# A graph layer on one NeuronCore: the next block's score chain moved forward in the edge stream, and the mixing work on k and v done tile by tile

## The reference, cut to what matters

```
# attention over edges, 4 heads of 64 features
z = s_self[:, edge_row] + s_neigh[:, edge_col]
e = where(z > 0, z, 0.2 * z) * adj_val
ex = exp(e - segment_max(e, edge_row)[edge_row])
alpha = ex / segment_sum(ex, edge_row)[edge_row]
out = relu(segment_sum(alpha * feat[edge_col], edge_row) + bias)
# mixing, 8 heads of 64
q, k, v = split(x @ w_qkv)
k, v = inst_norm(k), inst_norm(v)          # mean and variance over a head's 64 features
dots = einsum('bhnd,bhne->bhde', k, v)
mix = (einsum('bhnd,bhde->bhne', q, dots) / n) @ w_out + b_out
x = x + out + mix
```

## Time and profile before

| | |
|---|---|
| median of 3 runs | 2548.52 us |
| the profiled execution | 2553.18 us, its span 2551.4 us |
| weights of blocks 0 and 25 (exponents, L972) | at 615.71 and 1758.56 us |
| last add of the edge stream (L1387) | 1792.89 us |
| busy in the span | PE 1742.6, DVE 1735.7, ACT 1408.0, POOL 1367.9 us |
| mean granted TensorE clock | 0.801 |

### The profile page before, as it was taken

How to read it: one execution, slowest core, us unless ns; L and a number is a source line. 1 busy time by engine, 2 the same in 40 slices (tenths; PEclk the granted TensorE clock), 3 DMA queues, 4 the chain that set the end, 5 groups by cost and what they waited for, 6 DMA issues and landing times. The chain is left out here.

```text
span 2551.4 us, 39924 instructions
## 1 busy us (share of the span) xinstructions
PE 1742.6 (68%) x8110; PEld 1309.4 (51%) x8111; DVE 1735.7 (68%) x3888; ACT 1408.0 (55%) x4644; POOL 1367.9 (54%) x1293
## 2 busy tenths in 40 slices
PE   3788841146666656766676776767574699999965
PEld 1444421023444444544454454544464699999954
DVE  6988999974776766777766556566883344444468
ACT  2555543315767757768776865868441244444434
POOL 2444410017777666666777666660177466666521
PEclk9899975566766877777878787878555799999988
DMA  6333420025554544454655444440629233333354
GB/s 200 132 141 146 168 85 0 0 82 157 159 158 152 167 152 144 142 180 123 186 158 174 131 140 117 141 139 17 199 44 131 66 105 105 104 105 106 102 169 146
DMA packets 173333, 323.66 MB, mean 127 GB/s; under 512 B 34435, under 2 KB 108720, under 8 KB 173182
## 3 DMA queue, kind: packets, MB, share of 16 engines
q1 hardware_dynamic: 110750, 172.84, 21.0%
q0 software_dynamic: 54176, 140.57, 19.4%
q10 hardware_dynamic: 8256, 8.68, 1.7%
HBM read 248.04 MB, written 73.94 MB: 126 GB/s over the span
## 5 line engine op out<-in xcount | busy, mean ns | idle before, releaser
L953 POOL DMA_INDIRECT big<-feat_d,pair_idx x832 | 819.9, 985 | 360.2 <-issue 177.0
L980 ACT ACTIVATE big<-big 128x64 f32<-128x64 f32 x3328 | 800.3, 333 | 0.8
L1081 PE MATMUL wide<-big 128*128 128x260 f32 x1664 | 637.6, 510 | 105.4 <-DVE big L1387 87.0
L1387 DVE TENSOR_TENSOR big<-big,wide 128x260 f32 x832 | 352.1, 423 | 341.8 <-PE wide L1081 262.2
L1081 PEld LDWEIGHTS wide<-big 128*128 128x128 f32 x1664 | 351.8, 244 | 176.5 <-ACT big L980 110.2
L313 ACT ACTIVATE big<-big 128x896 f32<-128x896 f32 (+2 forms) x153 | 136.9, 895 | 170.1 <-DVE big L538 155.1
L2068 PEld LDWEIGHTS p_h<-xT,w_sb 128*128 128x128 f32 x1808 | 221.7, 194 | 5.7
L2068 PE MATMUL p_h<-xT,w_sb 128*128 128x128 f32 x1808 | 222.1, 277 | 0.0
L2079 PE MATMUL p_o<-w_sb,hT 128*128 128x256 f32 x904 | 213.9, 379 | 1.1 <-DVE w_sb L2017 1.1
L1958 POOL DMA_INDIRECT moe_d<-x_out,x_to x113 | 134.6, 1191 | 135.6 <-DVE x_idx L1997 95.7
L278 POOL TENSOR_SCALAR xn<-X,mean,rstd 128x256 f32<-128x256 f32 x49 | 97.7, 1994 | 188.3 <-PE p_t L616 154.3
(11 more groups left out here) (327 smaller groups left out, 2853.2 us busy)
## 6 DMA issues: line engine op xcount, KB each, us to landing
big<-code_d SPq DMA_DIRECT2D x52, 512.0 KB, 4.0
kv_d<-big SPq DMA_DIRECT2D x49, 512.0 KB, 2.7
X<-kv_d SPq DMA_DIRECT2D x12, 2048.0 KB, 11.5
big<-in_L_ffn_w_dram SPq DMA_DIRECT2D x32, 512.0 KB, 10.5
b_sb<-in_L_ffn_b_dram SPq DMA_DIRECT2D x113, 128.0 KB, 3.0
big<-feat_d,pair_idx POOLq DMA_INDIRECT x832
big<-moe_d SPq DMA_DIRECT2D x7, 1792.0 KB, 10.0
feat_d<-feat_sb SPq DMA_DIRECT2D x49, 130.0 KB, 2.7
```

The lines of the kernel that those rows point to most:

```text
L953: nc.gpsimd.indirect_dma_start(out=rows[:, n // SB % RB, n % SB, :], out_offset=None, in_=m["feat_d"], in_offset=bass.IndirectOffsetOnAxis ...
L980: ins = nc.scalar.activation(rows[:, b, s, cols], rows[:, b, s, cols], ACT.Copy, scale=rows[:, b, s, HF + h:HF + h + 1])
L1081: nc.tensor.matmul(sums[s % RING][:, 0:HF + H], onehot[:, s // GP % 2, s % GP, :], rows[:, b, s, :], start=True, stop=True).then_inc(summe ...
L1387: nc.vector.tensor_tensor(of, of, sums[s % RING][:, 0:HF + H], ALU.add).then_inc(added, 1)
```

## The change

The chain for block k+1 begins in block k at add 6 in place of add 22. With it move the steps of all three engines: PE's four transposing steps go behind sums 8, 13, 17 and 21 (before: 23, 25, 26 and 27), `head` on ACT goes from slot 12 to slot 4 and the squares from slot 6 to slot 12. `sum_self` is done a block earlier, at slot 25 of the block before. The sums of squares, the scaling of v and the wait of each dot product now go one tile at a time, each of the first two as up to four instructions at four places. `first_hot` is a new one-row one-hot, so that `turn_arg` no longer reads the large one-hot buffer. `carry_f` and `carry_b` now live in `pens`.

```
 # ACT step
-                scale(k, b, range(0, 6))
+                scale(k, b, range(0, 4))
+                if there(k + 1):
+                    head(k + 1)
+                scale(k, b, range(4, 12))
                 if products:
                     squares_of(k, b, turn)
-                scale(k, b, range(6, 12))
-                if there(k + 1):
-                    head(k + 1)
                 scale(k, b, range(12, SB))
 # PE
-                nc.tensor.matmul(p_arg[:, HS:HS + H], onehot[0:1, 0, 0, :], drop[:], start=True, stop=True)
+                nc.tensor.matmul(p_arg[:, HS:HS + H], first_hot[:], drop[:], start=True, stop=True)
-                if i == 0:
-                    pe.wait_ge(v_scaled, k + 1)
+                pe.wait_ge(v_scaled, k * DB + (i + 1))
-                    i = (s - 8) // 2
-                    if s % 2 == 0 and i in batch(k - 1):
-                        dots(k - 1, 1 - b, i)
+                    if s - 9 in batch(k - 1):
+                        dots(k - 1, 1 - b, s - 9)
-                    if s in (8, 11, 14) and (s - 8) // 3 < len(groups(k)):
+                    if s in (9, 12, 15) and (s - 9) // 3 < len(groups(k)):
 # PE step, in the loop over s, behind sum s, its look-ups and mixing
+                    if s == 8:
+                        turn_z(k + 1)
+                    elif s == 13:
+                        turn_ends(k + 1)
+                    elif s == 17:
+                        turn_carry(k + 1)
+                    elif s == 21:
+                        turn_arg(k + 1)
 # DVE
+                wait_turn(dve, arg_turned, k)
+                nc.vector.tensor_tensor(first_hot[:], lane_p[0:1, :], pair_rel[0:1, ds(k * SB, 1)].to_broadcast([1, P]), ALU.is_equal)
-                nc.vector.tensor_reduce(var[:, 0:n * 2 * MH], squares[:, 0:n, :].rearrange("p t (h o) -> p t h o", o=64),
-                                        AX, ALU.add).then_inc(var_made, 1)
+                nc.vector.tensor_reduce(var[:, heads], squares[:, i, :].rearrange("p (h o) -> p h o", o=64), AX, ALU.add).then_inc(var_made, 1)
+            def scale_v(k, b, i):
+                v = kv[:, b, i, INNER:].rearrange("p (h o) -> p h o", o=64)
+                nc.vector.tensor_tensor(v, v, rkv[:, i, :].unsqueeze(2).to_broadcast([P, MH, 64]), ALU.mult).then_inc(v_scaled, 1)
 # DVE mixing: roots ahead of add 1, scale_v(i) ahead of add 2 + i, sum_squares(i) ahead of add 16 + 2 i
 # DVE step
-                if more:
-                    sum_self(k + 1)
                 fade_row(k, tile)
-                adds(range(0, 8))
+                adds(range(0, 3))
+                if more:
+                    heads(k + 1)
+                adds(range(3, 6))
+                if more:
+                    scores(k + 1, 1 - b, turn + b)
+                adds(range(6, 8))
                 select(k, 2)
-                adds(range(8, 11))
+                adds(range(8, 10))
+                if more:
+                    local_max(k + 1)
+                adds(range(10, 11))
                 if later:
                     turn_hot(2 * k + 5)
-                adds(range(11, 16))
+                adds(range(11, 14))
+                if more:
+                    carries(k + 1)
+                adds(range(14, 16))
                 select(k, 3)
+                adds(range(16, 19))
+                if more:
+                    arguments(k + 1)
+                adds(range(19, 25))
+                if more:
+                    select(k + 1, 0)
+                if later:
+                    sum_self(k + 2)
...
```

More of the change, by code:

```diff
@@ L719, in edge_stream @@
     run_b = sb("run_b", [1, H * (SB + 1) + 1])
-    carry_f, carry_b = sb("carry_f", [1, H, SB]), sb("carry_b", [1, H, SB])
-    drop = sb("drop", [1, H])
+    carry_f, carry_b = [pens[:].rearrange("u d h s -> u d (h s)")[:, d, 0:HS].rearrange("u (h s) -> u h s", h=H) for d in range(2)]
+    drop, first_hot = sb("drop", [1, H]), sb("first_hot", [1, P])
     wide = [ps(f"wide{i}", [P, 1024]) for i in range(4)]
@@ L1062, in turn_carry, with add_up @@
                 wait_apart(pe, carry_made, k + 1, crossed)
[L1063 to L1064 removed]
+                nc.tensor.transpose(p_row[0:HS, 256:257], flat(carry_f), ident[0:1, 0:1])
+                nc.tensor.transpose(p_row[0:HS, 257:258], flat(carry_b), ident[0:1, 0:1]).then_inc(col_turned, 1)
             def turn_arg(k):
                 pe.wait_ge(drop_made, k + 1)
[L1068 removed]
                 wait_turn(pe, ex_made, 2 * k)
                 wait_apart(pe, arg_made, k + 1, crossed)
[L1071 removed]
+                nc.tensor.matmul(p_arg[:, HS:HS + H], first_hot[:], drop[:], start=True, stop=True)
                 nc.tensor.transpose(p_arg[:, 0:HS], arg[:], ident[:]).then_inc(arg_turned, 1)
[L1074 to L1084, removed]
+            def add_up(k, b, s):
+                n = k * SB + s
+                if s % GP == 0:
+                    pe.wait_ge(hot_made, k * (SB // GP) + (s // GP + 1))
+                pe.wait_ge(scaled, n + 1)
+                pe.wait_ge(added, n + 1)
+                nc.tensor.matmul(sums[s % RING][:, 0:HF + H], onehot[:, s // GP % 2, s % GP, :], rows[:, b, s, :],
+                                 start=True, stop=True).then_inc(summed, 1)
             def dots(k, b, i):
[L1088 to L1089 removed]
+                pe.wait_ge(v_scaled, k * DB + (i + 1))
                 for g in range(GRP):
@@ L1145, in step @@
                 more, later = there(k + 1), there(k + 2)
-                for half in range(2):
-                    lo = half * HB
-                    if later:
+                for s in range(SB):
+                    half, at = s // HB, s % HB
+                    if later and at == 0:
                         tile = tiles_of(mybir.EngineType.PE, (2 * k + (4 + half)) * (HB // PACK), HB // PACK)
[L1150 to L1154, removed]
-                if more:
[L1156 to L1166, removed]
+                    add_up(k, b, s)
+                    if later and at < HB // 2:
+                        look_up(k + 2, half, tile, (2 * at, 2 * at + 1))
+                    mixing(k, b, stage, s)
+                    if not more:
+                        continue
+                    if s == 8:
[6 more added lines that the diff above has]
+                        turn_arg(k + 1)
             def first(k):
@@ L1436, in mixing @@
                 if stage == "dots" or isinstance(k, int) and DOTS - 1 <= k <= DOTS:
[L1437 to L1441, removed]
+                    if not (isinstance(k, int) and k == 0):
+                        if s == 1:
+                            roots(k - 1)
+                        if s - 2 in batch(k - 1):
+                            scale_v(k - 1, 1 - b, s - 2)
+                    if not (isinstance(k, int) and k == DOTS):
+                        if s % 2 == 0 and (s - 16) // 2 in batch(k):
+                            sum_squares(k, (s - 16) // 2)
+                    elif s == 16:
                         dve.wait_ge(dots_done, DOTS - 1)
@@ L1445, in mixing @@
                 elif stage == "mix":
-                    if s in (11, 14, 17) and (s - 11) // 3 < len(groups(k)):
-                        add_mix(k, (s - 11) // 3)
+                    if s in (12, 15, 18) and (s - 12) // 3 < len(groups(k)):
+                        add_mix(k, (s - 12) // 3)
                 elif k == DOTS + 1:
@@ L1508, in _ @@
             turn_hot(4)
+            sum_self(1)
             dve.wait_ge(zeroed, 1)
```

55 lines of the change are left out of this document (22 added, 33 removed).

## The result

The changed kernel takes 2488.07 us (2487.8 to 2491.11) against 2550.53 in the runs beside it, a ratio of 0.975, 95% interval 0.973 to 0.978. The forecast was 2484. The profiled execution took 2488.27 us.

What follows compares the result with a forecast made beforehand. It took a closed circle of ACT, DVE and PE as the bound; 648 + 1030 + 16 = 1694 against 1758.6 us gave a gain of 64.6 us, 2488.6 profiled and a 2484 us median, range 2440 to 2528.

Steps and rivals of the forecast that it cites:

- The sum: Edge stream: scores of block 1 at 648, then 1030 us of periods and 16 us to block 25's weights at 1694.
- DVE's sum: DVE, blocks with k and v: 36.2 us busy plus idle time makes 42.9, with 1.6 for PE a 44.5 us period.
- A loop's turn: DVE in looped blocks: 2.06 us of issue every second block, 1.0 us a block.
- the low clock: PE's four dot products: 1.9 us each at the lower clock, about half the time, costing DVE 1.6 us a block.
- The tail: Block 25: weights follow its scores by 15 slots of about 1.07 us, 16 us; nothing changes behind them.
- The floor: POOL's gathers: at least 41.3 us a block with k and v, 40.3 without; level with DVE in the mixing blocks.
- the circle: ACT scales block k, DVE and PE finish the next chain only near its end, ACT starts again: 45.6 us a period.
- rival C: PE's transposes: uncovered waits for DVE, two per block, 7 us, make the kernel slower, 2652 us; chance 0.09.
- A: Rival: PE costs DVE nothing; periods of 42.9 and 40.3, gain 96 us, time 2452; chance 0.15.
- B: Rival: TensorE's clock becomes the bound, staying at the lower level; mean period 45.6, no change, 2548 us; chance 0.09.
- D: Rival: gathers at add 6 hold the early chain in each block; mean period 43.8, time 2505 us; chance 0.12.
- The signs: Stream: DVE's busy share 0.81, idle some 8 us, ACT's wait 9 us a block, some 20 us for block 1's gathers.

Runs made afterwards that it cites:

- e3: The changed kernel with both loops (blocks 2 to 9 and 16 to 21) written out; 2465.9 us, ratio 0.966.
- e4: The changed kernel with each sum of squares reading, and each scaling of v writing, only 2 of 64 features; 2452.0 us, ratio 0.961.
- e5: The changed kernel with only the even slots gathered from block 2 on; 2461.1 us, ratio 0.966.
- e2: The kernel before with sums of squares and scaling of v done tile by tile, the chain not moved; 2507.9 us, ratio 0.983.
- e11: The changed kernel with the chain half way: scores ahead of add 12, PE's transposes behind sums 14, 19, 23 and 27; 2452.0 us, ratio 0.960.
- e1: The changed kernel with sums of squares, scaling of v and its wait made whole again, the chain moved; 2508.3 us, ratio 0.982.
- e6: The changed kernel with PE's four transposes behind sums 6, 10, 14 and 19 in place of 8, 13, 17 and 21; 2540.5 us, ratio 0.995.

## Why the prediction was right, and where not

**The sum.** The median came out 4 us from the forecast, which is in part luck. The terms are off by up to 11 us and cancel, and so do two things that the sum took as fixed:

| term | predicted | measured |
|---|---|---|
| first scores of block 1 | 648.0 | 647.6 |
| 12 periods to the scores of block 13 | 534 (44.5) | 522.7 (43.6) |
| 12 more to those of block 25 | 496 (41.3) | 497.3 (41.4) |
| from there to its weights | 16 | 21.6 |
| weights of block 25 | 1694 | 1689.3 |
| from there to the last add | unchanged, 34.3 | 38.5 |
| behind the last add | unchanged, 758.5 | 758.8 |
| median less the profiled execution | -4.7 | -0.2 |

**DVE's sum.** For written-out blocks it was 41.9 (42.9 less the loop's 1.0) and 1.6 for PE, 43.5, and blocks 10 and 11 take 41.6. The term that was most wrong is the work: I had it rise from 35.0 to 36.2 us, and DVE is busy 34.8. The six more instructions did cost about what I said, by their own durations (four sums of 1.21 us for one of 4.41), but in the trace an instruction often starts just before its neighbour's end (an add runs from 1083.47 for 0.42 us, the next step starts at 1083.81), so the split did not lengthen the busy time. A loop's turn was too small: from one row I took 2.06 us of DVE's issue, while e3 shows 4.4 us a turn. DVE's part of it appears at 811.95 with 3.64 us of issue; e3, without loops, has no such wait:

```profile
811.95 0.42 DVE L1369 TENSOR_TENSOR big<-big,wide 128x256 f32 x1 [3.64 <-issue]
```

For the low clock I had all four dot products at the lower level about half the time. In blocks 2 to 11 it is only the first one or two of the four. Block 2's first and third, PE in order of time:

```profile
734.72 1.92 PE L1086 MATMUL wide<-X 128*128 128x128 f32 x8
...
738.25 1.05 PE L1086 MATMUL wide<-X 128*128 128x128 f32 x8
```

The granted clock was 0.52 over the first and 1.00 over the third. So my 1.9 us at the lower level was right, though it is not twice 1.05. At adds 10 to 13, right behind the dot products, DVE waits for PE 1.0 us in blocks 10 and 11 and 1.7 in blocks 1 to 11, close to my 1.6, but part of the 0.3 us gaps is in that, and no run separates the clock's share.

**The tail.** Fifteen slots at 1.07 us gave 16 where 21.6 were measured. In them DVE also stands idle for PE's sums behind the mixing's output, 2.45 us at 1678.01 and 1.70 at 1685.06. And "behind it nothing changes" was wrong by the 4.2 us of block 25.

**POOL.** The floor and the place of its binding were right (e4, e5). Splitting the scaling did not give POOL its time back evenly: one gather met three pieces in a row.

```profile
1084.68 2.36 POOL L953 DMA_INDIRECT big<-feat_d,pair_idx  x1 [0.30 <-PE wide L1079]
```

It lost 1.4 us in place of 1.99, close to my 1.3. (My upper bound was wrong by itself: four pieces of 0.65 us are 2.6, not 2.3.) The piece issued at 1082.87, into a gather that was already running, cost nothing. Over the whole stage POOL got nothing back: its 832 gathers took 819.1 us against 819.9 before (806.2 in e2, 802.7 in e11).

**What failed is the first step, the circle.** I wrote that the stream is bound by a closed circle through ACT and that the gain comes from the chain's leaving it, the tiles being "the second gain". e2 shows that 43 of the 63 us come without moving the chain, and e1 that 43 come without the tiles. What the chain's late place cost are DVE's waits at adds 28 to 31, some 3 us a block with the usual gaps in them, and they hang on PE's wait for DVE's chain steps: rival C's mechanism, already at work in the kernel before. The size came out because I did not price the circle; I priced what remains on DVE in the new order, and that sum does not ask where the old idle time was from.

**Rivals.** A did not come: its first periods of 42.9 were 43.5 and its last, 40.3, were 41.6. B did not happen: the clock was granted 0.73 in blocks 2 to 9 and 0.84 in blocks 13 to 24, so it did not stay at the lower level; what it costs the period no run isolates. C is real as a mechanism (e6), and the change lowers it instead of bringing it. D, the gathers' hold at add 6, is the one that I priced as small: a place of the chain that gives it room is worth 36 us (e11), though not all of that need be D.

**The signs.** DVE's busy share in blocks 1 to 11 was 0.79 against the 0.81 that I gave and the 0.72 that would have refuted me, its idle time 9.0 us a block against some 8, ACT's wait 9.6 us a block against 9. POOL hardly waited for PE up to block 5. DVE waited 14.4 us for block 1's gathers, not 20. None of these signs could tell the circle from its rival: e2 could.

## What to carry to other kernels

When engines work in step through a small ring, the longest wait need not be the bound: here ACT and DVE had the same 35 us of work a block, and ACT's 318.2 us of waiting fell by 51.7 when only DVE's steps were split (e2). Take work off one engine and see how much of it the period gives back (e4 for DVE, e5 for POOL), then count where that engine stands idle. Splitting the long steps gave 43 us of the 63 by itself. Place a step that can wait for a transfer late enough that the partners keep work for its whole wait, and early enough for what needs its result; as early as possible was 36 us worse than half way.

## What the runs showed of the hardware

A `tensor_tensor` with both inputs in SBUF (fp32) held up a gather's issue on GpSimd: 2.92 to 2.95 us in place of 0.95 for the nine gathers issued at the start of a 2.29 us instruction, 2.18 to 2.51 for three issued later into it, and 2.36 for one across three of 0.67. Gathers of 128 rows were 1.25 us apart at best (0.95 of work and a gap of 0.30), and the data of a block's last one released DVE 2.75 to 2.92 us after its issue began wherever DVE waited for it in the changed kernel, except in the last block, where it was 4.11. The turn of a long loop body cost 4.4 us of the stream in one loop and 3.7 in the other.
